# Windowed attention and FFN on one core: row sums taken by ScalarE ahead of the second scores, the denominators' matmuls left out, one projection piece behind each head

## The reference, cut to what matters

```
h   = layernorm(x)
q,k = rope(h @ wq.T), rope(ctx @ wk.T);  v = ctx @ wv.T
s   = (q_head @ k_head.T) * sqrt(32)            # 16 heads, |i-j| <= 128 only
o   = softmax(s) @ v_head
x   = x + o @ wo.T + wo_b
x   = x + W_out_q @ quant(gelu(quant(layernorm(x)) @ W_in_q + b_in)) + b_out
```

## Time and profile before

| | |
|---|---|
| median of 3 runs | 1176.55 us |
| profiled execution, its own time | 1176.49 us |
| its span in the trace | 1174.8 us |
| outside the span | 1.7 us |
| TensorE busy | 1135.5 us (97%) |
| VectorE busy | 946.8 us (81%) |
| ScalarE busy | 646.8 us (55%) |
| GpSimd busy | 375.7 us (32%) |
| granted TensorE clock, mean | 0.988 |

### The profile page before, as it was taken

How to read it: one execution, slowest core, us unless ns; L and a number is a source line. 1 busy time by engine, 2 the same in 40 slices (tenths; PEclk the granted TensorE clock), 3 DMA queues, 4 the chain that set the end, 5 groups by cost and what they waited for, 6 DMA issues and landing times.

```text
span 1174.8 us, 23540 instructions
## 1 busy us (share of the span) xinstructions
PE 1135.5 (97%) x7928; PEld 766.9 (65%) x7928; DVE 946.8 (81%) x2413; ACT 646.8 (55%) x1033; POOL 375.7 (32%) x540
## 2 busy tenths in 40 slices
PE   6999999999999999999999789999999999999998
PEld 6867887887788788778878464444444444444443
DVE  6879989999999999999998756666666687777776
ACT  5255356436534643563464255555555577777774
POOL 1247337534743663474365230000000021111121
PEclk9989999999999999999999799999999999999999
DMA  8554674566457556646753723555553402676662
GB/s 281 133 150 114 172 221 118 148 184 163 126 175 212 129 137 184 172 123 179 203 139 92 222 65 118 197 196 198 196 196 117 152 1 77 214 232 227 224 216 99
DMA packets 100522, 191.10 MB, mean 163 GB/s; under 512 B 13376, under 2 KB 30912, under 8 KB 100416
## 3 DMA queue, kind: packets, MB, share of 16 engines
q1 hardware_dynamic: 96096, 179.92, 50.9%
q10 hardware_dynamic: 4320, 9.83, 2.8%
HBM read 89.16 MB, written 43.91 MB: 113 GB/s over the span
## 4 chain that ended last, share of the span: by engine, by line
PE 44%; DVE 26%; issue 25%; DMA 2%; ACT 1%; SPq 1%; DVEq 0%; POOL 0%; POOLq 0%; ACTq 0%
PE bank L864 19%; DVE bank L1224 12%; PE bank L642 6%; PE bank L656 5%; PE bank L669 5%; DVE row_max L1224 3%; PE bank L589 3%; PE bank L593 2%; DVE neg_max L1265 2%; DVE roped L1250 2%; DVE rt L1248 2%; DVE rt L1247 1%; DVE neg_max L1229 1%; DVE t_lo L1257 1%; PE bank L608 1%
## 5 line engine op out<-in xcount | busy, mean ns | idle before, releaser
L1224 DVE CUSTOM_DVE_ANT_0 bank<-bank,mask 128x256 f32<-128x256 f32 x512 | 203.5, 453 | 33.9 <-PE bank L608 23.1
L864 PE MATMUL bank<-wout_int,g_hi 128*128 128x512 bf16 x512 | 193.6, 379 | 0.1
L864 PE MATMUL bank<-wout_int,g_lo 128*128 128x512 bf16 x512 | 193.6, 379 | 0.0
L825 PE MATMUL bank<-qT_hi,win_int 128*128 128x512 bf16 x496 | 188.0, 379 | 0.0
L825 PE MATMUL bank<-qT_lo,win_int 128*128 128x512 bf16 x496 | 188.0, 379 | 0.0
L973 ACT ACTIVATE probs<-bank 128x512 f32<-128x512 f32 x256 | 139.0, 599 | 37.0 <-PE bank L642 31.1
L1542 POOL TENSOR_TENSOR k_lo<-roped,k_hi 128x256 fp32r<-128x256 f32 x60 | 55.0, 947 | 263.5 <-ACT k_hi L913 263.5
L1520 DVE TENSOR_TENSOR g_lo<-h_int,g_hi 128x512 f16<-128x512 f32 x128 | 89.1, 696 | 41.3 <-ACT g_hi L1129 37.4
L1565 POOL TENSOR_SCALAR_AFFINE_SELECT probs<-probs 128x256 f32<-128x256 f32 x256 | 107.1, 429 | 35.9 <-ACT probs L973 30.0
L1097 ACT ACTIVATE h_ring<-bank,b_in,g_scale 128x512 f32<-128x512 f32 x96 | 73.1, 779 | 71.2 <-PE bank L825 56.4
L1462 DVE TENSOR_REDUCE hmax<-h_ring 128x512 f32 (+1 forms) x96 | 63.1, 682 | 58.5 <-ACT h_ring L1097 56.4
(11 more groups left out here) (170 smaller groups left out, 2735.0 us busy)
## 6 DMA issues: line engine op xcount, KB each, us to landing
hidden_scratch<-h_ring SPq DMA_DIRECT2D x96, 256.0 KB, 2.1
h_ring<-hidden_scratch SPq DMA_DIRECT2D x96, 256.0 KB, 2.9
k_st<-k_hi SPq DMA_DIRECT2D x128, 128.0 KB, 2.9
q_st<-q_hi SPq DMA_DIRECT2D x128, 128.0 KB, 2.7
xq<-x_scratch SPq DMA_DIRECT2D x16, 1024.0 KB, 6.0
x_ln<-in_x SPq DMA_DIRECT2D x16, 512.0 KB, 6.3
ctx_raw<-in_ctxT SPq DMA_DIRECT2D x16, 512.0 KB, 5.0
k_st<-k_lo SPq DMA_DIRECT2D x64, 128.0 KB, 2.8
```

Source lines behind the costliest of these rows:

```text
L825: mm = pe.matmul(bank[f % 4][:], win_int[:, c, f * P:(f + 1) * P], part[:, par, c], start=c == 0 and part is qT_hi, stop=c == KC - 1 and p ...
L864: return pe.matmul(bank[4 * par + u][:], part[:, f % 4, u * P:(u + 1) * P], wout_int[:, f], start=f == 0 and part is g_hi, stop=f == FC - ...
L1224: dve.tensor_tensor_reduce(sc, sc, mask[:, (1 - qb) * P:(1 - qb) * P + S], 1.0, NEG, ALU.add, ALU.max, row_max[:, qb, n:n + 1]).then_inc(m ...
```

## The change: what it does

- The query weights are scaled by -sqrt(32) on loading, so the scores come out negated and scaled. The row maxima become row minima (`row_minima`), computed in place in PSUM.
- Behind the minima of a head ScalarE takes exp(minimum - score) of both halves, in place, with an accumulated sum for each row (`row_sums`: 32 ACTIVATE instructions of 256 columns in each step). The bank is free for the next head only after that.
- After head 15 ScalarE takes the logarithm of the sums and one exponential for a correction (`logs`), VectorE makes minimum and log-sum into one shift in five small operations (`log_sums`), and that is transposed in place of the maximum. So the exponentials of phase 2 are normalised probabilities, and `denominators`, `invert`, `normalise`, the two DMAs of a step and the shares at the end are gone.
- One projection piece stands behind each head. Two of v's eight chunks move into phase 2, and all products of the output projection but six move ahead of the first `scores_t`: three each behind heads 13 and 14, twelve behind head 15, four behind the transposes, one each after `scores_t` 4 and 6.
- Bank 6 takes the scores of heads 12 and 15 (`early`, `ahead`); the transposes of the shift go to bank 6 in place of bank 7.
- VectorE's work between the heads is cut finer: quantising W_in behind heads 0 to 2 (before: in phase 2), the low parts of the transposed x behind heads 4 and 5, one operation of k's `rotate` behind each of heads 6 to 11. The high part of k is copied by GpSimd (`k_lead`) in place of ScalarE, the low part of q is one operation of VectorE (`q_low`) in place of four of GpSimd.

```diff
--- before.py
+++ after.py
...
@@ -190,16 +187,16 @@
+        early = [bank[i] for i in (0, 1, 0, 1, 0, 1, 0, 1, 0, 1, 0, 1, 6, 0, 1, 6)]
+        ahead = [max([m for m in range(n) if early[m] is early[n]], default=None) for n in range(H)]
...
@@ -595,29 +589,33 @@
                 if n < 2:
                     wait(pe, exp_done, H * b)
+                elif ahead[n] is not None:
+                    pe.wait_ge(sum_done, 2 * (H * b + ahead[n] + 1))
+                elif has_proj:
+                    pe.wait_ge(v_done, 2 * (b + 2) - 1)
                 else:
-                    pe.wait_ge(max_done, 2 * (H * b + n - 1))
+                    wait(pe, oT_out, 2 * b - 1)
...
@@ -729,29 +711,30 @@
                 if has_proj:
-                    tiles[1] += [lambda: qk_tile(b + 1, "k", 0)]
-                    tiles[3] += [lambda: x_transposes(b + 1, 0), lambda: x_transposes(b + 1, 1), lambda: qk_tile(b + 1, "k", 1, (0,))]
...
+                    for n, (which, half, col) in {0: ("k", 0, 0), 1: ("k", 0, 1), 3: ("k", 1, 0), 4: ("k", 1, 1),
+                                                  7: ("q", 0, 0), 8: ("q", 0, 1), 9: ("q", 1, 0), 10: ("q", 1, 1)}.items():
+                        tiles[n] += [lambda which=which, half=half, col=col: qk_tile(b + 1, which, half, (col,))]
+                    tiles[2] += [lambda: x_transposes(b + 1, 0), lambda: x_transposes(b + 1, 1)]
+                    tiles[5] += [lambda: v_tile(b + 1, 0, range(2))]
+                    tiles[6] += [lambda: v_tile(b + 1, 0, range(2, KC))]
+                    tiles[11] += [lambda: v_tile(b + 1, 1, range(1))]
+                    tiles[12] += [lambda: v_tile(b + 1, 1, range(1, 2))]
+                for n in (13, 14):
+                    tiles[n] += [lambda: some(3)]
...
-                some(7)
+                some(12)
                 max_transposes(b, has_proj)
                 some(4)
-                for n, count in enumerate((1, 2, 2, 2, 1, 1, 1, 0, 1, 1, 0, 0, 1, 0, 0, 0)):
+                for n in range(H):
                     scores_t(b, n, has_o, has_proj)
-                    some(count)
+                    if n in (0, 2) and has_proj:
+                        v_tile(b + 1, 1, range(2 + n // 2, 3 + n // 2))
+                    if n in (4, 6):
+                        some(1)
...
@@ -943,7 +914,9 @@
             def ot_lead(j, s, has_q):
-                act.wait_ge(onorm, 2 * (j + 1) if j < NB - 1 else 2 * j + s + 1)
+                act.wait_ge(oT_out, 2 * (j + 1))
...
@@ -980,14 +953,24 @@
+            def row_sums(b, n):
+                if n == 0:
+                    wait(act, lse_chain, LSE_OPS * b)
+                act.wait_ge(min_done, 2 * (H * b + n + 1))
+                for qb in range(2):
+                    sc = early[n][:, qb * S:(qb + 1) * S]
+                    act.activation(sc, sc, ACT.Exp, scale=-1.0, bias=row_min[:, qb, n:n + 1],
+                                   accum_out=row_sum[:, qb, n:n + 1]).then_inc(sum_done, 1)
+
+            def logs(b):
+                act.wait_ge(sum_done, 2 * H * (b + 1))
+                act.activation(lse[:], row_sum[:], ACT.Ln).then_inc(log_done, 1)
+                act.wait_ge(log_done, 2 * b + 1)
+                act.activation(lse_e[:], lse[:], ACT.Exp, scale=-1.0).then_inc(log_done, 1)
...
@@ -1021,27 +1004,26 @@
+                for n in range(H):
+                    row_sums(b, n)
+                    if n == 3 and has_proj:
+                        xt_lead(b + 1, 0)
+                        xt_lead(b + 1, 1)
+                    if n == 7 and has_proj:
+                        v_copy(b + 1, 1 - par, 0)
+                    if n == 11 and has_o:
+                        ot_lead(b - 1, 0, has_proj)
+                        ot_lead(b - 1, 1, has_proj)
+                logs(b)
                 max_copy(b, 0, slice(0, 2))
                 max_copy(b, 0, slice(2, KC))
                 for n in range(H):
                     softmax_exp(b, n)
-                    if n == 6 and has_proj:
+                    if n == 4 and has_proj:
+                        v_copy(b + 1, 1 - par, 1)
+                    if n == 5 and has_xt:
+                        ctx_hi(b + 2)
+                    if n == 7 and has_proj:
                         split_hi("q", b + 1)
...
@@ -1336,36 +1331,41 @@
+                between = [[] for _ in range(H)]
+                window = quantise_win(b)
+                for n in (0, 1, 2):
+                    between[n] += [lambda: next(window, None)]
                 if has_proj:
...
+                    first, second = rotate(b + 1, "k", 0), rotate(b + 1, "k", 1)
+                    between[4] += [lambda: xt_rest(b + 1, 0)]
+                    between[5] += [lambda: xt_rest(b + 1, 1)]
+                    for n in (6, 7, 8):
+                        between[n] += [lambda: next(first, None)]
+                    for n in (9, 10, 11):
+                        between[n] += [lambda: next(second, None)]
                 for n in range(H):
...
+                    row_minima(b, n)
+                    for work in between[n]:
+                        work()
+                log_sums(b)
...
@@ -1541,6 +1532,12 @@
+            def k_lead(j):
+                pool.wait_ge(rope_step["k"], ROPE_OPS * (j + 1))
+                for i in range(NC4):
+                    wait(pool, stacked["k"][i], STAGED * j)
+                pool.tensor_copy(part_hi["k"][:], roped[:]).then_inc(hi_done["k"], 1)
+
...
@@ -1571,22 +1568,19 @@
             def step(b, par, has_c, has_o, has_proj, has_xt):
+                if has_o:
+                    bias_x(b - 1)
                 if has_proj:
+                    k_lead(b + 1)
                     for c in range(KC):
                         split_lo("k", b + 1, c)
                 if has_o:
                     ot_rest(b - 1, 0)
                     ot_rest(b - 1, 1)
...
                 for n in range(H):
                     band(b, n)
-                    if 6 <= n < 10 and has_proj:
-                        split_lo("q", b + 1, n - 6)
-                    if n in (1, 3) and has_xt:
-                        ctx_lo(b + 2, n // 2 + 2)
+                    if 8 <= n < 12 and has_xt:
+                        ctx_lo(b + 2, n - 8)
```

More of the change, by code:

```diff
@@ L74, in constants @@
     q, k = np.arange(S)[:, None], np.arange(S)[None, :]
-    mask = folded(folded(np.where(np.abs(q - k) <= WINDOW, 0.0, NEG).astype(np.float32), 0), 1)
+    mask = folded(folded(np.where(np.abs(q - k) <= WINDOW, 0.0, FAR).astype(np.float32), 0), 1)
     assert not mask[:P, :P].any() and not mask[P:, P:].any()
     mask = np.concatenate([mask[P:], mask[:P, P:]], 1)
-    hot = np.tile((np.arange(HOT) % NC4 == NC4 - 1).astype(np.float32), (P, 1))
-    row, col = np.arange(P)[:, None], np.arange(P)[None, :]
-    pick = np.stack([row == DK * (col // DK) + i for i in range(NC4)], 1).astype(np.float32)
     sel = np.zeros((P, H), np.float32)
@@ L596, in o_products, with scores @@
                         yield
-            def scores(b, n):
+            def scores(b, n, has_proj):
                 if n % KC == 0:
@@ L644, in scores_t, with weighted @@
                 mm.then_inc(st_mm, 1)
-            def weighted(b, par, i, kb):
+            def weighted(b, par, i, kb, has_proj):
                 if kb == 0:
@@ L659, in weighted @@
                     mm.then_inc(pv_mm, 1)
-            def denominators(b, i, kb, has_proj):
-                if i == 0 and kb == 0:
-                    wait(pe, den_done, b)
-                    if has_proj:
-                        pe.wait_ge(rope_step["q"], ROPE_OPS * (b + 2))
-                one_hot = hot[:, NC4 - 1 - i:NC4 - 1 - i + DK]
-                for c in range(KC):
-                    n = KC * i + c
-                    mm = pe.matmul(den_bank[DK * c:DK * (c + 1), 0:S], one_hot, probs[:, n % SLOTS, kb],
-                                   start=i == 0 and kb == 0, stop=i == NC4 - 1 and kb == 1)
-                if kb == 1:
-                    mm.then_inc(den_mm, 1)
             def clump(b, par, i, has_proj):
                 for kb in range(2):
-                    weighted(b, par, i, kb)
-                for kb in range(2):
-                    denominators(b, i, kb, has_proj)
+                    weighted(b, par, i, kb, has_proj)
             def w_transposes(b, has_proj):
@@ L761, in _ @@
             steps(pe, step)
-            def last_shares():
-                pe.wait_ge(pick_in, 16)
-                pe.wait_ge(exp_done, H * NB)
-                for s in range(2):
-                    pe.wait_ge(den_done, NB + s)
-                    for i in range(NC4):
-                        mm = pe.matmul(ring[s][:, i * P:(i + 1) * P], pick[:, i], den_r[:, s * P:(s + 1) * P],
-                                       start=True, stop=True)
-                    mm.then_inc(share_mm, 1)
             def last_products():
@@ L1252, in rotate, with turn, q_low @@
                 dve.wait_ge(s, base + 3)
+            def turn(*args):
```

(25 more changed lines are left out.)

176 lines of the change are left out of this document (60 added, 116 removed).

## The result

The changed kernel takes 1280.59 us (median of 4 runs, 1278.42 to 1284.21), the kernel before beside it 1176.99 (1173.67 to 1179.10): a ratio on record of 1.0897, 95% interval 1.0873 to 1.0920 (the two medians divide to 1.0880). It is about 9% slower. The profiled execution took 1284.21 (span 1282.5), 107.7 more than the profiled one of before. By the transposes of the maxima, now of the shift, these divide so: 8.9 before the first (60.62, now 69.57), 96.9 in the next fourteen intervals, 4.6 in the last, -2.8 behind it.

What follows compares the result with a forecast made beforehand. TensorE was taken to bound both phases, VectorE close behind. The profiled 1176.5 us + 96 (steps 1 to 14) + 7 (step 0) - 2 (the end) = 1277, + 18 for the clock = 1295; range 1230 to 1350.

Steps and rivals of the forecast that it cites:

- Phase 1: First score matmul to the transposes of the shift: 24.3 us of TensorE work plus waits, 31.3 against 24.2.
- k_lead: GpSimd's copy of k's high part, ahead of the output's low part: priced 1.5 us, from 1.06 to 3.0.
- The pair of sums: ScalarE's two row-sum ACTIVATEs for one head: priced 1.0 us, bounds 0.7 and 1.2.
- The log-sum chain: Small operations after head 15: done at 30.1, at latest 31.2, covered by products until the transposes at 31.3.
- Phase 2: Transposes to the next step: GpSimd's bands end it at 16.4 us against 16.6, despite 3.9 less TensorE work.
- Steps 1 to 14: Steady steps at full clock: 47.7 us each against 40.8, +96 us in all.
- The clock: Clock falls after the stalls at head 5 and the ninth product: a quarter of 28 at 2.6 us, +18.
- Step 0: First step, without output products: the log-sum chain stands bare behind head 15, 29.4 against 22.6, +7 us.
- Step 15 and the end: Last step: phase 1 about 25 us against 22, phase 2 shorter by 2, final shares gone; together -2.
- Rival B: The clock falls at nearly every stall: 1277 + 28 x 2.6 = 1350 us; chance 0.15.
- Rival C: Shorter waits at k_lead, row sums and head 5: 44.3 us a step, 1230 us; chance 0.15.
- Rival D: Low parts arrive before TensorE asks, so its work decides: 36.9 us a step, 1115 us; chance 0.06.

Runs made afterwards that it cites:

- short sums: Kernel after with each row-sum ACTIVATE over 32 of its 256 columns, constants for scale and bias, softmax not normalised: 1278.1 us, ratio 1.0887.
- that run: Kernel after with GpSimd's two t_lo (attention output's low part) ahead of k's high and low parts instead of behind them: 1299.47 us, ratio 1.1076.
- The later runs: Kernel after with its streams laid anew in several rounds, lastly q's low part and W_in's rows earlier: 1186.98, 1227.17, 1195.44, then 1171.23 us.
- the two forms of phase 2: Rearranged kernel of 1187 us with phase 2 laid anew: q's high part behind exponential 3, clumps moved, 1227.17 us; behind exponential 5, clumps back, 1195.44 us.

## Why the prediction was right

- **Phase 1, 31.3 predicted:** 29.9. Waits were forecast at 6.9 and are 4.3. At v's first chunk 2.3 was forecast and 1.93 came; at the first product 1.2 and 0.89; at the ninth 2.6 and 1.60. The 0.8 at heads 2 and 4 didn't come: no wait of 0.2 or more stands there. TensorE's own work was forecast at 24.3 and is 25.6, 1.3 more. About 0.8 of it stands at the three waits: the matmul ahead of each counts as busy 0.17 beyond its usual spacing (430.63 + 0.41), and the one behind it holds up the next by 0.1 (0.31 from 432.97, 0.23 later). The rest is a gap of 0.2 ahead of head 2 and three heads that take 0.32 to 0.35 where the earlier trace rows had 0.24.
- **k_lead:** 1.5 taken from 1.06 to 3.0; it is 1.04, just under the lower end. It starts 22.3 us into phase 1 at full clock (444.77 after 422.49; 23.1 forecast). So `ot_lo` comes at 27.5 (29.0 forecast), while TensorE asks at 25.8 (26.4): most of the 1.0 by which the wait on it was too long.
- **The pair of sums:** 1.0 taken; 0.91. With short sums the time moved by 2.5 us, where -8 to +7 was allowed.
- **The log-sum chain** was forecast to be covered, by 1.1 at worst by nothing, and to give back 1.1 to 1.5 without the stall. It is covered by 0.3 us (404.73 against 405.03). Without the stall it gave back all of it and more: a wait of 2.00 in place of 1.60, 0.3 a step at full clock, and more falls of the clock. I had let one small operation wait for GpSimd; in that run three did.
- **Phase 2, 16.4 predicted:** 16.6 at full clock, ended by GpSimd's bands as forecast. Band 8 starts 9.3 after the transposes (9.2 forecast for its exponential). Less work of TensorE shortens the 16.6 of the earlier trace rows by nothing here, since GpSimd's order took over.
- **Steps 1 to 14, +96 at full clock:** +96.9 in the trace, but that holds the clock. At full clock it would be 14 x (46.63 - 40.82) = +81, so the steps were forecast 15 us too long, and that 96 stands beside 96.9 is chance.
- **The clock, +18:** +15.6 by the run with matmuls in the waits. The size was right by luck, for its two factors were not: I had 7 falls at 2.6; the trace shows one in each of 13 steps, at 1.6 around head 5 (31.57 - 29.93) and 0.9 at the turn (17.46 - 16.60). They stand around head 5 (first row) or at the turn of a step (second row), never at the wait on `ot_lo`:

```profile
143.90:153.90 10.00, 8.91 (x50) 8.03 (x51) 5.56 (x22) 4.87 (x19) 2.51 (x2) 0.83 0.30 106
418.40:422.50 4.10, 3.91 (x37) 1.42 (x37) 2.01 (x4) 1.54 (x3) 2.19 (x6) 0.58 0.87 207
```

  In the second the last clump takes 1.85 us in place of the earlier trace rows's 0.89. Matmuls in the waits shorten no wait, and 15.6 us go. The Trainium skill (TensorE: Matmul & The Clock Gate, The HAM clock gate) says that the default is throttled and activity releases it; the trace agrees.
- **Step 0, +7:** +8.9, with 3.73 of TensorE's idle time ahead of its transposes. **Step 15 and the end, -2:** +1.8 (4.6 - 2.8). In step 15 a head takes 1.47, half of it waiting for the sums, at a clock near a half; the 25 forecast for it left the clock out. The two misses are +1.9 and +3.8.
- **The sum:** 1295 against 1284.2 profiled and 1280.6 median. The steps were 15 us too long, the clock 2, the ends 6 too short.
- **Rival B** (a fall at nearly every stall): partly so. One a step, not two, at less than half the price. **Rival C** (shorter waits): k_lead (1.04) and the wait at head 5 (1.93) came as it had them; the pair of sums (0.91) and phase 2 (16.6, not 15.0) did not, and its step of 44.3 is further from 46.6 than the forecast's 47.7. **Rival D** (TensorE's work decides): not at the order written. The later runs reach 40.2, not its 36.9. A clump followed by scores takes 1.00 in place of 0.89, so four clumps without denominators free 3.5 us and not the 3.9 of the prediction. In phase 2, 13.6 long, ScalarE is busy for 12.5 with its 16 exponentials and the copies between them; that it is the bound there fits and was not tested.

## What to carry to other kernels

Work taken from the engine that is busy all the time is worth what the next wait leaves of it, and count it by the spacing in the timeline and not by the number of instructions (here 14 of 16 records gave 0.46 of 0.98 us). Moving it to two other engines costs wherever an in-order queue has something else in front: read where the consumer asks, not how busy the producer is. The 9% was such an order: the same computation with its streams laid otherwise ran in 1171 us. Two waits that stand one behind the other hide each other, so take both away or neither, and after each move look at what the queue that was filled (transfers included) now delivers late. A stall of about 2 us in a stream of matmuls can be paid again through the clock; if it must stay, matmuls without a reader inside it are a cheap cure (1.2% here).

## What the runs showed of the hardware

- An ACTIVATE with a row sum is followed by an ACTIVATION_READ_ACCUMULATOR of 202 ns, which adds only some 0.09 us to the spacing of 0.45 for 256 columns (an estimate: at 397.27 an ACTIVATE starts, at 397.62 its reading, at 397.72 the next instruction). With 32 columns the pair of instructions takes 258 and 199 ns.
- A one-operand copy of 128x1024 fp32 takes GpSimd 1.04 us, where its subtraction of two operands takes 0.75 for 128x256.
- VectorE's operations of 32 columns with two SBUF operands take 0.19 us alone and 0.52 to 0.91 beside a GpSimd subtraction. A rotation's last operation went from 0.69 to 1.15 beside the context's low parts in the two forms of phase 2. A rule of the Trainium skill (SBUF — State Buffer, Who interferes with whom) says this of a VectorE instruction with two SBUF inputs and a GpSimd instruction that reads SBUF; the trace agrees, and it gives the price: up to 0.72 us for an operation of 0.19.
- The granted clock fell after waits of 1.6 to 2.0 us within dense work (0.66 over the 5 us after one of 1.63), and at the turn of a step after shorter ones (1.2 for a clump), but never at the wait on `ot_lo` of 1.60. With the short sums that wait is 1.96, and there it fell once in fourteen steps (0.66 from 493 to 498). What sets the difference stays open.
- Sixteen matmul records of shape 128*32 take 0.98 us ahead of scores, and two of them still 0.52 (the kernel before, with all and with two of a clump's denominator records).
